# Head of a two-layer graph kernel on one core: where codes, casts, weights and the staging of h stand

## The chip, the cores and the metric

The kernel runs on one core of a Trainium2 chip. The metric is device time in microseconds, the median of three runs: 883.71 us (883.47 to 884.96). Engines are named as in the profile: PE (TensorE), DVE (VectorE), ACT (ScalarE), POOL (GpSimd) and SP, which only issues DMAs. SPq and ACTq are the DMA issues of SP and of ACT.

## The reference

4,096 nodes with 256 features, a 4096x4096 adjacency of zeros and ones, two graph layers, each followed by a residual and a layernorm:

```python
def reference(x, adj, ...):
    deg = jnp.maximum((adj != 0).astype(jnp.float32).sum(-1), 1.0)
    # layer 0: a_norm = (adj + I) scaled by deg on both sides; relu((a_norm @ x + x) @ W + b)
    x = _layernorm(x + _L0_gnn_ref(x, adj, deg[..., None], W, b), axis=-1)
    # layer 1: sums of neighbours, two sigmoid gates, attention over neighbours, second product with adj
    x = _layernorm(x + _L1_gnn_ref(x, adj, adj, W_sa, a_sa, W_gcnb, b_gcnb, Wa, ba, Wb, bb), axis=-1)
    return x
```

## The kernel before, in words

The 4,096 nodes are T = 32 tiles of 128. The change lies in the first third of the kernel, which ends at about 340 us of the span: layer 0 and the projections for layer 1. Nothing behind it is edited but two waits.

**Strips and codes.** The adjacency is read as 128 strips of 512 KB, 16 to a panel of 512 columns (eight panels). SP issues each strip into a ring of RING = 6 buffers; strip s waits for the cast of strip s-6. ACT (line 509) or DVE (line 791) casts a strip to 8-bit codes; `on_act(s)` says which. The codes of a panel, 2 MB, are later written to HBM by `codes_when_cast` (line 329), for layer 1. Before, they are issued when strip 16q+21 has been issued. SP is one queue in order: what stands behind a waiting issue waits too.

**The t loop (t = 0 to 32).** For each tile PE transposes x (`xt_step`, line 1334), multiplies the tile before it with W0 (`z_step`, line 1349), and from t = 14 adds one row block into all four sums of panel 0 (`pass0_rows`, eight matmuls of line 1366). ACT copies the transposes (`xt_copy`, line 517), the first twelve z and makes the high part of y (line 529). DVE copies the other z (line 804) and makes the low part (line 831). Before that DVE needs the largest |x| (`x_max`, line 798, one reduction for each chunk of x), from which the scale `sx_ready` comes. At t = WT_AT PE transposes `wrow` (line 1422), which waits for all ten small weight DMAs. At t = WNORM_AT PE adds the squared weights (line 1415), and DVE takes the norm (`weight_norm`).

**The sums.** After the t loop PE finishes tiles 0 to 3 with the remaining rows (128 matmuls), then does tiles 4 to 31, four to a panel: each is 64 matmuls of line 1366 in four quarters (`sum_tile`). Between the quarters stand one transpose of an earlier tile's x1 (`t_step`, line 1386) and one projection (`p_step`, line 1401, twelve matmuls). The first tile of a panel walks through all 16 of its strips.

**The tile chain.** DVE turns a finished sum into x1 (`degree`, `residual`, `stats`, `normalize`), with POOL for the power. After the projection ACT evicts q, g and the high part of h (`proj_copies`, lines 563 to 577), DVE makes the low part (`h_lo`, line 933) and ACT issues the tile's h to HBM (line 557). h is staged in `hst`, two buffers before the change: `proj_copies(n)` waits for the write of h(n-2) with `act.wait_ge(h_out[n % 2], ...)`. `p_step(n)` waits for `h_lo(n-1)`. All engines run their instructions in the order in which they are written.

**Casts between the tiles.** The t loop of ACT casts at each odd t from 11, that of DVE at each even t from 12. Then come three casts each, then single ones between the first tiles, and from n = 6 two on each engine per tile.

Of the kernel before, what the change touches and what calls it, by code (L numbers as in the profile page):

```python
# [14 lines left out]
P = 128  # L15
N = 4096
D = 256
T = N // P
# [15 lines left out]
WT_AT = 16  # L34
WNORM_AT = 23
WTS_AT = 4
WARM = 20
# [24 lines left out]
XCUT = (0, 2, 4, 8, 16, 24, 32)  # L62
# [28 lines left out]
def build(nc, x, adj, W0, b0, Wsa, asa, Wg, bg, Wa, ba, Wb, bb, out):  # L91
# [78 lines left out]
    hst = area("hst", [P, 2, 2, ROW], F16)  # L170
# [45 lines left out]
    with ExitStack() as ctx:  # L216
# [24 lines left out]
        panel_in, slb_in, h_out = (several(name, 2) for name in ("panel_in", "slb_in", "h_out"))  # L241
# [22 lines left out]
        on_act = lambda s: s % 2 == 0  # L264
# [17 lines left out]
        def h_place(n):  # L282

            return hst[:, n % 2] if n < T - 2 else fb[:, n]
# [23 lines left out]
        def _(sp):  # L308
# [23 lines left out]
            sp.dma_start(w0[:], W0.rearrange("(k p) d -> p k d", p=P)).then_inc(S["w0_in"], 16)  # L332
            for c in range(1, len(XCUT) - 1):
                t0, t1 = XCUT[c], XCUT[c + 1]
                sp.dma_start(xs[:, t0:t1, 0:D], x_view[:, t0:t1, :]).then_inc(x_in[c], 16)  # L335
            for s in range(NSTRIP):
                if s >= RING:
                    sp.wait_ge(S["cast_act" if on_act(s - RING) else "cast_dve"],
                               casts_until(s - RING)[0 if on_act(s - RING) else 1])
                qq, g = s // GS, s % GS  # L340
                sp.dma_start(strip[:, s % RING], adj_view[:, g * SJ:(g + 1) * SJ, qq * 2 * PW:(qq + 1) * 2 * PW]  # L341
                             ).then_inc(strip_in[s % RING], 16)
                if s == WTS_AT:
                    load_weights()
                if s >= RING and (s - RING) % GS == GS - 1:
                    codes_when_cast((s - RING) // GS)
# [19 lines left out]
            for c in range(NCH):  # L366
                upto = min((c + 1) * CH, T - 2)
                for i in range(2):
                    sp.wait_ge(h_out[i], 16 * upto // 2)
                sp.dma_start(fb[:, c * CH:upto].rearrange("p t k c -> p t (k c)"), hd[:, c * CH:upto, :]  # L370
                             ).then_inc(fb_in[c], 16)
# [124 lines left out]

        ACT_CASTS = [s for s in range(NSTRIP) if on_act(s)]
# [4 lines left out]
        def _(act):  # L502
# [27 lines left out]

            for t in range(T):
                xt_copy(t)
                if 1 <= t <= ZACT:
                    z_copy(t - 1)
                for i in split_at(t):
                    y_hi(i)
                if t >= 11 and t % 2 == 1:
                    cast(1)
# [13 lines left out]
            def proj_copies(n):  # L552

                t, p = n, n // 2
                if 0 < n < T - 1:
                    act.wait_ge(S["hlo_ready"], n)
                    act.dma_start(hd[:, n - 1, :], hst[:, (n - 1) % 2].rearrange("p k c -> p (k c)")
                                  ).then_inc(h_out[(n - 1) % 2], 16)
# [15 lines left out]
                if 2 <= n < T - 2:  # L574
                    act.wait_ge(h_out[n % 2], 16 * (n // 2))
# [12 lines left out]
            cast(3)  # L588
            x1t_copy(0)
            cast(1)  # L590
# [187 lines left out]
        def _(dve):  # L778
# [116 lines left out]
            z_scale()  # L895
            for t in range(ZACT, T):
                if t == WT_AT:
                    gate_columns()
                if t == WNORM_AT:
                    weight_norm()  # L900
                z_copy(t)
                for i in split_at(t):
                    y_lo(i)
                if t % 2 == 0:
# [7 lines left out]
                if t >= T - 4 and t % 2:  # L912
                    weight_parts((t - T + 4) // 2)
            for t in split_at(T):
                y_lo(t)
            cast(3)
# [93 lines left out]
            cast(1)  # L1010
            first_head(2)
            cast(2)
# [263 lines left out]
            for i in range(2):  # L1276
                dve.wait_ge(h_out[i], 16 * (T - 2) // 2)
# [141 lines left out]

# [211 lines left out]
```

## Time and profile before

| | us |
|---|---|
| median of three runs | 883.71 |
| the profiled execution, own time | 886.22 |
| its span | 884.1 |
| PE busy in the span | 859.0 |
| DVE busy | 670.8 |
| ACT busy | 570.6 |
| mean granted clock of PE | 0.992 |

The span runs from the first to the last instruction that the profiler recorded; the execution's own time is 2.1 us longer. Busy PE time is modelled from pipelined matmuls, so the stretches in which PE waits are the more telling reading. The rows below are read in this order: who PE waits for in the first third, at what clock it goes on, the order of time on PE, DVE and ACT, and what the DMA engines move in the same stretches.

### The profile page before, as it was taken

The page shows a single profiled execution, that of the slowest core. Times are in us where ns is not written, and L with a number is a line of the kernel's source. Part 1 is how long each engine was busy: PE and PEld are TensorE (multiplying, and loading weights), DVE is VectorE, ACT ScalarE, POOL GpSimd, SP SyncE. Part 2 cuts the span into 40 slices and gives each one's busy share as a digit, 9 for nine tenths or more (in the row PEclk, how much of TensorE's full clock was granted, in tenths as well). Part 3 has the DMA queues.
Part 4 walks back from the last instruction along what each step waited for, and adds up shares of the span by engine and source line. Part 5 has one row for each costly group of instructions (what it writes and reads, how often), then busy time and mean ns, then how long its engine had stood idle before and what let it go on. Part 6 is the DMA issues. An engine that isn't in the chain of part 4 may idle for free.

```text
span 884.1 us, 20460 instructions
## 1 busy us (share of the span) xinstructions
PE 859.0 (97%) x7579; PEld 756.9 (86%) x7579; DVE 670.8 (76%) x1182; ACT 570.6 (65%) x1214; POOL 178.2 (20%) x181
## 2 busy tenths in 40 slices
PE   8899799999999999999999999999999999999997
PEld 7778688888888887888788888888888888888886
DVE  5686566565666557998889988978978978879863
ACT  5663455454555327889877967967867867867831
POOL 1001233222232220110122022032032032032021
PEclk9999999999999999999999999999999999999999
DMA  9879799989989615101220220220220220220001
GB/s 319 286 263 324 256 397 381 373 302 342 357 300 365 234 42 212 57 5 52 78 79 1 77 77 0 77 77 0 77 77 0 77 77 0 77 77 0 25 25 36
DMA packets 66617, 130.01 MB, mean 147 GB/s; under 512 B 5464, under 2 KB 29056, under 8 KB 62080
## 3 DMA queue, kind: packets, MB, share of 16 engines
q1 hardware_dynamic: 57632, 120.87, 38.8%
q10 hardware_dynamic: 8928, 8.38, 2.8%
q8 instruction: 36, 0.59, 0.3%
q14 instruction: 21, 0.17, 0.1%
HBM read 99.87 MB, written 29.36 MB: 146 GB/s over the span
## 4 chain that ended last, share of the span: by engine, by line
PE 82%; DVE 5%; issue 4%; ACT 4%; SPq 2%; DMA 1%; POOL 0%; POOLq 0%; DVEq 0%; ACTq 0%
PE ps L1530 31%; PE ps L1366 25%; PE ps L1471 19%; PE ps L1401 5%; ACT ec L624 2%; DVE ec L1100 1%; PE ps L1349 1%; ACT em L633 1%; DMA sc<-in_L_gnn_bb_dram 1%; PE ps L1386 1%; SPq L341 1%; DVE em L1107 1%; SPq L335 1%; DVE dd L940 0%; DMA x1r<-x_scratch 0%
## 5 line engine op out<-in xcount | busy, mean ns | idle before, releaser
L1530 PE MATMUL ps<-fb,em 128*128 128x257 f16 x3072 | 347.5, 273 | 0.8 <-DVE em L1107 0.8
L1530 PEld LDWEIGHTS ps<-fb,em 128*128 128x128 f16 x3072 | 300.4, 98 | 38.6 <-issue 1.3
L1366 PE MATMUL ps<-y,codes 128*128 128x257 f16 x2048 | 238.4, 274 | 1.7 <-DVE codes L791 1.3
L1366 PEld LDWEIGHTS ps<-y,codes 128*128 128x128 fp8e4 x2048 | 200.6, 98 | 29.2 <-DVE codes L791 1.6
L624 ACT ACTIVATE ec<-slb,nsb 128x256 f32<-128x256 f32 x512 | 211.1, 496 | 0.0
L1107 DVE SCALAR_TENSOR_TENSOR em<-ec,em 128x2048 f16<-128x2048 f32 x64 | 147.4, 2303 | 22.7 <-ACT em L633 22.7
L633 ACT ACTIVATE em<-ec 128x2048 f16<-128x2048 f32 x64 | 122.0, 1908 | 65.4 <-PE ps L1530 57.2
L1100 DVE SCALAR_TENSOR_TENSOR ec<-ec,pan 128x2048 f32<-128x2048 f32 x64 | 147.3, 2301 | 2.6 <-issue 1.8
L1471 PE MATMUL ps<-zz,dd 128*128 128x256 f16 x768 | 89.4, 273 | 1.5 <-DVE t L1129 1.3
L458 POOL TENSOR_TENSOR sc<-sc,sc 128x2 f32<-128x2 f32 x15 | 38.5, 2569 | 246.2 <-DVE sc L1209 246.2
L1471 PEld LDWEIGHTS ps<-zz,dd 128*128 128x128 fp8e4 x768 | 75.0, 98 | 10.7 <-issue 2.0
L509 ACT ACTIVATE codes<-strip 128x1024 uint8<-128x1024 f32 x64 | 65.4, 1048 | 18.5 <-DMA strip<-in_adj_dram 17.5
L1471 PE MATMUL ps<-fa,pan 128*128 128x260 f16 x512 | 61.7, 279 | 3.4 <-DVE s L1138 2.1
L452 POOL TENSOR_TENSOR w<-w,bgb 128x512 f32<-128x512 f32 x16 | 27.7, 1732 | 184.6 <-DVE w L1167 184.6
L940 DVE SCALAR_TENSOR_TENSOR dd<-pan 128x512 uint32<-128x512 uint32 (+2 forms) x85 | 64.1, 814 | 0.0
L1471 PEld LDWEIGHTS ps<-fa,pan 128*128 128x128 fp8e4 x512 | 50.7, 99 | 11.7 <-issue 2.3
L1471 PE MATMUL ps<-fa,dd 128*128 128x260 f16 x512 | 59.6, 274 | 0.4 <-DVE m L1119 0.4
L1471 PEld LDWEIGHTS ps<-fa,dd 128*128 128x128 fp8e4 x512 | 49.9, 98 | 7.6 <-issue 0.9
L548 ACT ACTIVATE x1t<-ps 128x256 f16<-128x256 f32 x32 | 12.2, 382 | 66.0 <-PE ps L1386 66.0
L1401 PE MATMUL ps<-wps,x1t 128*128 128x256 f16 (+1 forms) x384 | 48.9, 278 | 4.1 <-issue 4.1
L791 DVE TENSOR_SCALAR codes<-strip 128x1024 uint8<-128x1024 f32 x64 | 43.8, 688 | 11.8 <-DMA strip<-in_adj_dram 11.8
L956 DVE TENSOR_SCALAR lnst<-ps 128x1 f32<-128x1 f32 x32 | 5.0, 156 | 60.7 <-PE ps L1366 60.6
(154 smaller groups left out, 765.1 us busy)
## 6 DMA issues: line engine op xcount, KB each, us to landing
strip<-in_adj_dram SPq DMA_DIRECT2D x128, 512.0 KB, 7.5
a_scratch<-codes SPq DMA_DIRECT2D x16, 1024.0 KB, 10.6
pan<-a_scratch SPq DMA_DIRECT2D x16, 1024.0 KB, 4.9
x_scratch<-x ACTq DMA_DIRECT2D x32, 128.0 KB, 5.2
x1r<-x_scratch SPq DMA_DIRECT2D x16, 256.0 KB, 2.8
h_scratch<-hst ACTq DMA_DIRECT2D x30, 136.0 KB, 5.4
out_dram<-ot SPq DMA_DIRECT2D x15, 256.0 KB, 2.2
fb<-h_scratch SPq DMA_DIRECT2D x3, 1088.0 KB, 8.7
```

The source lines that it names most:

```text
L458: pool.tensor_tensor(sc1[:, RS2], sc1[:, VE2], sc[:, MH2], ALU.pow).then_inc(S["yrstd_ready"], 1)
L509: act.activation(codes_of(s), strip_of(s), ACT.Copy, scale=float(EDGE - NONE), bias=float(NONE)).then_inc(S["cast_act"], 1)
L624: e_ = act.activation(ec[:, c % ER, jj, :], slb[:, slot, :], ACT.Exp, scale=-(1 - SLOPE), bias=nsb[:, jb:jb + 1])
L633: act.activation(em[:, c, 0], ec[:, c % ER], ACT.Copy, scale=MU / EDGE_VAL).then_inc(S["ehigh_ready"], 1)
L791: dve.tensor_scalar(codes_of(s), strip_of(s), float(EDGE - NONE), float(NONE), ALU.mult, ALU.add).then_inc(S["cast_dve"], 1)
L940: return dve.scalar_tensor_tensor(out=o, in0=b, scalar=0x7f7f7f7f, in1=a, op0=ALU.bitwise_and, op1=ALU.bitwise_xor)
L1100: dve.scalar_tensor_tensor(out=ec[:, c % ER], in0=ec[:, c % ER], scalar=1.0, in1=pan[:, slot, c * CH:(c + 1) * CH, :].bitcast(F8), op0=ALU ...
L1107: dve.scalar_tensor_tensor(out=em[:, c, 1], in0=ec[:, c % ER], scalar=MU / EDGE_VAL, in1=em[:, c, 0], op0=ALU.mult, op1=ALU.subtract).then ...
L1366: mm = pe.matmul(ACC(n), codes[:, qq % SLOTS, h, jb, e * P:(e + 1) * P].bitcast(F8), y[:, jb, part, 0:YC], start=(jb == 0 and part == 0), ...
L1401: mm = pe.matmul(b, x1t[:, n % 2, x_part, k * P:(k + 1) * P], wps[:, k, w_part, c0:c1], start=(k == 0 and x_part + w_part == 0), stop=(k = ...
L1471: mm = pe.matmul(ps[:, bank, 0:2 * c], a.bitcast(F8), g, start=(p == 0), stop=(p == NP - 1))
L1530: mm = pe.matmul(PH(2 * m + e)[:, 0:HC], em[:, c, e_part, i, e * P:(e + 1) * P], fb[:, jb, h_part, 0:HC], start=(jb == 0 and e_part + h_pa ...
```

## The change

Eight things are altered, all in the head:

1. The warm-up transposes go from 20 to 15, and x comes in eight chunks instead of six (the first two of one tile, the last two of four). W0's DMA is issued by ACT instead of SP.
2. `wrow`'s transpose and the weight steps behind it move from t = 16 to t = 20, the weight norm from t = 23 to t = 27. On DVE `gate_columns` and `weight_norm` move ahead of the casts of their tile.
3. ACT takes the odd strips, DVE the even ones, and ACT also all of strips 26 to 31. The casts of the t loops follow two lists: ACT at t = 13, 15, 19, 21 to 31, DVE once before the loop and at t = 14, 16, 20, 22 to 30.
4. After the t loops DVE casts four strips with `weight_parts(1)` between them, and none between the first heads; ACT casts seven, then two and one.
5. The codes of panel 0 are issued after strip 32 instead of 21, those of panel 1 after strip 43 instead of 37. The later ones stay at 16q+21.
6. `hst` has three buffers, and the waits and writes follow.
7. The waits at the end of the head for the h writes cover three semaphores.
8. The layout of the area of `hst`, `gb` and `fs` grows by one buffer.

```diff
-WT_AT = 16
-WNORM_AT = 23
+WT_AT = 20
+WNORM_AT = 27
-WARM = 20
+WARM = 15
+HRING = 3
+BOTH_AT = 26
-XCUT = (0, 2, 4, 8, 16, 24, 32)
+XCUT = (0, 1, 2, 4, 8, 16, 24, 28, 32)
-    hst = area("hst", [P, 2, 2, ROW], F16)
+    hst = area("hst", [P, HRING, 2, ROW], F16)
-        on_act = lambda s: s % 2 == 0
+        on_act = lambda s: s % 2 == 1 or BOTH_AT <= s < 2 * GS
...
-            sp.dma_start(w0[:], W0.rearrange("(k p) d -> p k d", p=P)).then_inc(S["w0_in"], 16)
+            CODES_AT = [2 * GS, 2 * GS + GS // 2 + RING // 2] + [q * GS + GS + RING - 1 for q in range(2, NQ - 1)]
-                if s >= RING and (s - RING) % GS == GS - 1:
-                    codes_when_cast((s - RING) // GS)
+                if s in CODES_AT:
+                    codes_when_cast(CODES_AT.index(s))
...
+        ACT_AT, DVE_AT = (13, 15, 19, 21, 23, 25, 27, 29, 31), (14, 16, 20, 22, 24, 26, 28, 30)
+            act.dma_start(w0[:], W0.rearrange("(k p) d -> p k d", p=P)).then_inc(S["w0_in"], 16)
-                if t >= 11 and t % 2 == 1:
+                if t in ACT_AT:
                     cast(1)
...
-                if 2 <= n < T - 2:
-                    act.wait_ge(h_out[n % 2], 16 * (n // 2))
+                if HRING <= n < T - 2:
+                    act.wait_ge(h_out[n % HRING], 16 * (n // HRING))
...
-            cast(3)
+            cast(7)
             x1t_copy(0)
-            cast(1)
+            cast(2)
             x1t_copy(1)
...
             z_scale()
+            cast(1)
             for t in range(ZACT, T):
-                if t == WT_AT:
+                z_copy(t)
+                if t == WT_AT - 1:
                     gate_columns()
-                if t == WNORM_AT:
-                    weight_norm()
-                z_copy(t)
                 for i in split_at(t):
                     y_lo(i)
-                if t % 2 == 0:
+                if t == WNORM_AT - 1:
+                    weight_norm()
+                if t in DVE_AT:
                     cast(1)
...
-                if t >= T - 4 and t % 2:
-                    weight_parts((t - T + 4) // 2)
+                if t == T - 1:
+                    weight_parts(0)
             for t in split_at(T):
                 y_lo(t)
-            cast(3)
+            cast(2)
+            weight_parts(1)
+            cast(2)
...
             first_head(1)
-            cast(1)
             first_head(2)
-            cast(2)
             first_head(3)
```

On PE, in the t loop, `xs` is x, `w_94` is W0 and `wrow` holds the rows of the gate weights. Before, the transpose of `wrow` is the sixth step of this piece, right behind the second row block of panel 0:

```order
L1366 MATMUL ps<-y,codes 128x257 x8
L1334 MATMUL ps<-ident,xs 128x128 x2
L1349 MATMUL ps<-w_94,xt 128x256 x2
L1422 MATMUL ps<-ident,wrow 128x8
L1366 MATMUL ps<-y,codes 128x257 x8
L1334 MATMUL ps<-ident,xs 128x128 x2
```

Now the same piece stands four tiles later:

```order
L1372 MATMUL ps<-y,codes 128x257 x8
L1340 MATMUL ps<-ident,xs 128x128 x2
L1355 MATMUL ps<-w_94,xt 128x256 x2
L1427 MATMUL ps<-ident,wrow 128x8
L1372 MATMUL ps<-y,codes 128x257 x8
L1340 MATMUL ps<-ident,xs 128x128 x2
```

Only its place moved: six row blocks of panel 0 stand ahead of it instead of two.

On SP, the issue of panel 0's codes (`a_scratch`) before, behind strip 21:

```order
L341 DMA strip<-in_adj_dram 128x2x512 [waits cast_act]
L341 DMA strip<-in_adj_dram 128x2x512 [waits cast_dve]
L329 DMA a_scratch<-codes 128x8192 [waits cast_dve,cast_act]
L329 DMA a_scratch<-codes 128x8192
L341 DMA strip<-in_adj_dram 128x2x512 [waits cast_act]
```

And now, behind strip 32 (the row "x2" is strips 31 and 32, the row "x5" strips 33 to 37):

```order
L344 DMA strip<-in_adj_dram 128x2x512 [waits cast_dve]
L344 DMA strip<-in_adj_dram 128x2x512 [waits cast_act] x2
L332 DMA a_scratch<-codes 128x8192 [waits cast_dve,cast_act]
L332 DMA a_scratch<-codes 128x8192
L344 DMA strip<-in_adj_dram 128x2x512 [waits cast_act] x5
L344 DMA strip<-in_adj_dram 128x2x512 [waits cast_dve]
```

Ten strips of panel 1 and the first one of panel 2 have moved ahead of the 2 MB, and strips 33 to 37 wait for ACT alone.

On ACT, from the last steps of the t loop to the second tile, before:

```order
L529 ACTIVATE y<-zf,sc 128x256 [waits zf_dve] x2
L509 ACTIVATE codes<-strip 128x2x2x256 [waits strip_in4]
L509 ACTIVATE codes<-strip 128x2x2x256 [waits strip_in0]
L509 ACTIVATE codes<-strip 128x2x2x256 [waits strip_in2]
L548 ACTIVATE x1t<-ps 128x256 [waits x1t_done]
L550 DMA x_scratch<-x_61 128x256 [waits x1_ready]
L509 ACTIVATE codes<-strip 128x2x2x256 [waits strip_in4]
```

And now:

```order
L533 ACTIVATE y<-zf,sc 128x256 [waits zf_dve] x2
L513 ACTIVATE codes<-strip 128x2x2x256 [waits strip_in1]
L513 ACTIVATE codes<-strip 128x2x2x256 [waits strip_in3]
L513 ACTIVATE codes<-strip 128x2x2x256 [waits strip_in5]
L513 ACTIVATE codes<-strip 128x2x2x256 [waits strip_in1]
L513 ACTIVATE codes<-strip 128x2x2x256 [waits strip_in2]
L513 ACTIVATE codes<-strip 128x2x2x256 [waits strip_in3]
L513 ACTIVATE codes<-strip 128x2x2x256 [waits strip_in4]
L553 ACTIVATE x1t<-ps 128x256 [waits x1t_done]
L555 DMA x_scratch<-x_61 128x256 [waits x1_ready]
L513 ACTIVATE codes<-strip 128x2x2x256 [waits strip_in5]
L513 ACTIVATE codes<-strip 128x2x2x256 [waits strip_in0]
```

Four more casts (strips 19 to 28 in all) stand ahead of the copy of the first transposed x1, and two instead of one behind it.

## Rows read from the trace of the kernel before

**Rows 1.** Waits of PE, 0 to 330 us: line, releaser, total, times, longest.

```profile
PE ps L1401 <- issue: 4.1, 1, 4.1
PE ps L1422 <- DMA sc<-in_L_gnn_bb_dram: 2.7, 1, 2.7
...
PE ps L1366 <- DVE codes L791: 1.3, 1, 1.3
PE ps L1349 <- ACT xt L517: 1.0, 3, 0.4
PE ps L1386 <- DVE x L990: 0.9, 1, 0.9
PE ps L1415 <- DVE zf L804: 0.5, 1, 0.5
PE ps L1366 <- DVE y L831: 0.4, 1, 0.4
```

**Rows 2.** Windows: stretch, length, five engines' busy time, granted clock, DMA, GB/s.

```profile
30.60:34.00 3.40, 3.40 (x14) 2.55 (x12) 0.08 (x1) 1.29 (x3) 0.00 (x0) 0.50 0.95 358
102.30:105.70 3.40, 2.89 (x14) 2.05 (x15) 3.12 (x10) 0.10 (x1) 0.72 (x1) 0.51 0.30 112
```

**Rows 3.** PE in order of time: start, length, instruction, [idle before <- releaser].

```profile
1.78 4.53 PE L1325 MATMUL ps<-ident 128*128 128x128 f32 x20 [1.78 <-POOL ident L416]
...
29.99 0.22 PE L1422 MATMUL ps<-ident,wrow 8*128 8x8 f32 x1 [2.74 <-DMA sc<-in_L_gnn_bb_dram]
...
34.68 0.38 PE L1334 MATMUL ps<-ident,xs 128*128 128x128 f32 x2
...
36.64 0.38 PE L1334 MATMUL ps<-ident,xs 128*128 128x128 f32 x2
...
102.81 2.75 PE L1401 MATMUL ps<-wps,x1t 128*128 128x262 f16 x12 [4.06 <-issue]
...
108.38 0.44 PE L1386 MATMUL ps<-ident,x 128*128 128x128 f32 x2 [0.95 <-DVE x L990]
...
129.35 1.49 PE L1401 MATMUL ps<-wps,x1t 128*128 128x262 f16 x12
```

**Rows 4.** DVE in time: the last x reduction, tile 6's low x1t.

```profile
16.90 2.29 DVE L798 TENSOR_REDUCE sc<-xs 128x1 f32<-128x2048 f32 x1 [0.58 <-DMA xs<-in_x_dram]
...
126.44 0.42 DVE L946 SCALAR_TENSOR_TENSOR x1t<-ps,x1t 128x256 f16<-128x256 f32 x1
```

**Rows 5.** ACT and its DMA issues in time, around two waits.

```profile
90.59 0.64 ACTq L557 DMA_DIRECT2D h_scratch<-hst  x1
...
101.56 0.20 ACT L576 ACTIVATE hst<-q 128x1 f16<-128x1 f32 x1 [4.23 <-DMA h_scratch<-hst]
...
121.64 1.06 ACT L509 ACTIVATE codes<-strip 128x1024 uint8<-128x1024 f32 x1 [1.93 <-DMA strip<-in_adj_dram]
```

**Rows 6.** Windows, the last two numbers: DMA share and GB/s.

```profile
35.00:40.00 5.00, 5.00 (x36) 4.22 (x35) 4.24 (x13) 3.88 (x9) 0.00 (x0) 1.00 0.62 221
...
80.00:90.00 10.00, 8.68 (x79) 7.50 (x78) 7.95 (x25) 2.85 (x9) 2.58 (x5) 1.00 0.76 245
...
100.00:110.00 10.00, 6.24 (x43) 4.80 (x44) 6.36 (x18) 4.93 (x12) 2.89 (x5) 0.83 0.45 151
110.00:120.00 10.00, 10.00 (x94) 8.90 (x92) 6.78 (x21) 5.97 (x14) 1.82 (x3) 1.00 1.02 378
```

**Rows 7.** The page, part 6: DMA issues, count, size, median us to landing.

```profile
strip<-in_adj_dram SPq DMA_DIRECT2D x128, 512.0 KB, 7.5
a_scratch<-codes SPq DMA_DIRECT2D x16, 1024.0 KB, 10.6
...
h_scratch<-hst ACTq DMA_DIRECT2D x30, 136.0 KB, 5.4
```

**Rows 8.** Waits of SP's queue, 0 to 330 us: who held strips.

```profile
SPq L341 <- ACT codes L509: 136.3, 36, 10.5
```

**Rows 9.** SP's queue in order of time: the codes of panel 1.

```profile
88.59 0.98 SPq L329 DMA_DIRECT2D a_scratch<-codes  x2
```

More of the change, by code:

```diff
@@ L240, in build @@
         codes_out, x1_out = several("codes_out", SLOTS), several("x1_out", X1RING)
-        panel_in, slb_in, h_out = (several(name, 2) for name in ("panel_in", "slb_in", "h_out"))
+        panel_in, slb_in = (several(name, 2) for name in ("panel_in", "slb_in"))
+        h_out = several("h_out", HRING)
         fb_in, x1r_in, out_sent = several("fb_in", NCH), block_sem("x1r_in"), block_sem("out_sent")
@@ L282, in h_place @@
         def h_place(n):
-            return hst[:, n % 2] if n < T - 2 else fb[:, n]
+            return hst[:, n % HRING] if n < T - 2 else fb[:, n]
         def differences(slot, op, p0, p1):
@@ L367, in _ @@
                 upto = min((c + 1) * CH, T - 2)
-                for i in range(2):
-                    sp.wait_ge(h_out[i], 16 * upto // 2)
+                for i in range(HRING):
+                    sp.wait_ge(h_out[i], 16 * len(range(i, upto, HRING)))
                 sp.dma_start(fb[:, c * CH:upto].rearrange("p t k c -> p t (k c)"), hd[:, c * CH:upto, :]
@@ L556, in proj_copies @@
                     act.wait_ge(S["hlo_ready"], n)
-                    act.dma_start(hd[:, n - 1, :], hst[:, (n - 1) % 2].rearrange("p k c -> p (k c)")
-                                  ).then_inc(h_out[(n - 1) % 2], 16)
+                    act.dma_start(hd[:, n - 1, :], hst[:, (n - 1) % HRING].rearrange("p k c -> p (k c)")
+                                  ).then_inc(h_out[(n - 1) % HRING], 16)
                 act.wait_ge(S["proj_done"], n + 1)
@@ L1275, in _ @@
             read_52(0, first=True)
-            for i in range(2):
-                dve.wait_ge(h_out[i], 16 * (T - 2) // 2)
+            for i in range(HRING):
+                dve.wait_ge(h_out[i], 16 * len(range(i, T - 2, HRING)))
             add_52(0, first=True)
```

## The prediction, made before the changed kernel was run

> **What bounds the kernel now.** I read the waits of PE first, since PE is busy for 859 of 884 us and nothing can be won that is not one of its waits, its clock, or work that it is spared. In the first 330 us PE waits seven times for something that the change touches [rows 1]: 4.1, 2.7, 1.3, 1.0, 0.9, 0.5 and 0.4 us. From 110 us on PE is busy without a gap up to 330 us (the last window of [rows 6] is the first such one), so the change can be worth only what stands ahead of 110 us, and whatever is saved there must not come back as a wait behind it. The second view is the granted clock: after each of the two long waits it falls to 0.5 (1.2 GHz) for 3.4 us [rows 2], and after that it is back at 1.0. The third is the order of time on PE, DVE and ACT, which says what each wait is made of.
>
> The 4.1 us stand as "issue" on PE, but PE was held by p_step(3), which needs h_lo(2). ACT had done everything up to the eviction of h(2) and stood 4.23 us before 101.56 waiting for the write of h(0) out of the same buffer [rows 5]. That write was issued at 90.59 and needed 10.9 us, where the 30 writes have a median of 5.4 [rows 5, 7]; 2 MB of panel 1's codes had been issued 2 us before it [rows 9].
>
> **The change, part by part.** Each gain below is for PE, which sets the end here.
>
> *Warm-up and x.* Twenty transposes take 4.53 us, or 0.227 each [rows 3]; five fewer are 1.1 us. W0 leaves SP's queue, and the first x chunk is half as large, so x is there. But the first y waits for the largest |x|, whose last reduction (8 tiles, 2.29 us) starts at 16.90 when x has landed [rows 4]. Two chunks of four tiles take half of it each; the first runs mostly while the second lands, but it starts behind the 2.29 us of the chunk before, so about 0.4 us is saved there. ACT's order then also loses a cast ahead of the first y. The gain at the first row block lies between 0.4 and 1.1; I take **0.8**, nearer the upper end because one of ACT's short waits (0.4, [rows 1]) lies in the same place.
>
> *The weights.* PE idles 2.74 us before `wrow`'s transpose, for a DMA landing at 29.99 [rows 3], and the half clock from 30.60 costs another 3.4 / 2 = 1.7 [rows 2]. A step of the t loop is 36.64 - 34.68 = 1.96 us [rows 3]. Four steps later and 0.8 earlier, the transpose is reached at 29.99 - 2.74 - 0.8 + 4 x 1.96 = 34.3 us. The weights keep their place in SP's queue with the same bytes ahead of them, so they land near 30: a cover of 4.3 us. Gain 2.7 + 1.7 = **4.4** (4.0 to 4.4).
>
> *The weight norm.* The step from the squares to the norm's matmul is three tiles as before, so the 0.5 us on line 1415 [rows 1] stays. What followed it (0.4 on the next z, [rows 1], since DVE did a cast before the norm) goes: **+0.4** (0 to 0.6). At the end of the loop ten small weight instructions of DVE now stand three tiles from the end instead of seven, ahead of the low y on which PE already waits 0.4 [rows 1]. I put **-0.3** (-1.0 to +0.4).
>
> *Codes of panel 0 and the casts.* 2 MB at 378 GB/s [rows 6, 7] are 5.5 us of the DMA engines, a strip is 1.39. Ten strips of panel 1 now pass ahead of them. The casts of the t loop free the buffers at the loop's own pace, so I expect these strips some 6 us earlier than before, which is also by how much PE comes earlier (0.8 + 4.4 + 0.4 - 0.3 = 5.3): they are neither the gain nor the loss. The 1.3 us that PE waits for a cast of DVE [rows 1] stem from two DVE casts behind the third head. These go to ACT, whose last one (strip 31) stands behind one x1t copy and `proj_copies(0)`. I estimate its end 2.9 us behind the end of t_step(1) (a cast is 1.06 [rows 5], the copies before it under 2); PE needs it after 28 of 32 matmuls at 0.11, 3.1 us behind. Cover 0.2 us. Gain **1.3** (0.5 to 1.3).
>
> *The ring of three.* `proj_copies(2)` waits no more. The write of h(0) is then asked for only by `proj_copies(3)`, one projection and 64 matmuls later. The wait of 4.06 goes and with it the half clock that made twelve matmuls take 2.75 us where they take 1.49 [rows 3]: 4.06 + 1.3 = **5.4** (4.0 to 5.5). Next late is what stands now: the 0.95 before t_step(4) [rows 3], DVE's chain of head(4) and h_lo(3). With a shorter p_step(3) DVE's part ends relatively later: **-0.3** (-1 to 0).
>
> Sum so far: 0.8 + 4.4 + 0.4 - 0.3 + 1.3 + 5.4 - 0.3 = 11.7 us.
>
> *What comes back: the DMA engines.* Panel 2's strips have to be there 11.7 us sooner, and from 110 to 120 us the engines are at a share of 1.02 [rows 6]. Before, the last cast of ACT for panel 2 starts at 121.64 when its strip lands [rows 5]; DVE's is one strip later, 123.0. The bytes up to that strip are the same after the change. What can be made up is idle time of the engines: against 378 GB/s, 221 over 35 to 60 us (taking the row shown for the 25 us) is 10.4 us idle, 245 over 80 to 90 is 3.5, 151 over 100 to 110 is 6.0: 20 us. After: two strips a step of the loop are 1.05 MB in 3.93 us = 267 GB/s, so some 24 us x 0.29 = 7 idle there, and about 3 where strip 38 waits for DVE's cast of strip 32, which stands behind forms_lo(0). So 20 - 10 = 10 us are made up, and the last strip lands at 113.2 (110.5 to 116.5). It is now ACT's. From the start of ACT's last cast to the low x1t of tile 6 it took 126.86 - 121.64 = 5.2 us [rows 4, 5], with a little waiting in it: 5.0. So p_step(6), which needs that, can start at 118.2; without any wait it would start at 129.35 - 11.7 = 117.65 [rows 3]. Taking also the writes of x1 and h that fall between, I put **-1.2** (0 to -4). After that the engines gain on PE: a panel is 16 x 1.39 + 5.5 + 2.9 for x1 and h = 30.6 us against 34.3 of PE (four tiles of 64 matmuls, a projection and a transpose, 8.6 each). The steady casts wait little; SP waits for casts for 136.3 us [rows 8], not casts for SP.
>
> Net 11.7 - 1.2 = 10.5 us, which shifts the whole rest of the kernel. The profiled execution took 886.22 with a span of 884.1; the median of the runs is 883.71, and the sum is a difference, so it goes to the median: **873.2 us**.
>
> A rule weighed against it. Row: the write of h(0), on ACT's queue, landed 10.9 us after its issue, behind codes on SP's queue [rows 5, 9]. The Trainium skill, DMA: Bandwidth & Descriptors, section Queues, rings and completion order, says that each DMA engine round-robins between queue rows by the packet, and by that alone the write would have taken the usual 5.4 us, nobody would have waited, the ring would gain nothing, and the sum would be 10.5 - 5.4 = 5.1, or 878.6; the trace disagrees, with 10.9 us. The same section says that a semaphore's increment lands only behind every earlier write of that engine across its queues; the trace agrees, and by it the sum stays at 10.5.
>
> **The rivals.**
>
> *A: no time comes back* (the strips land as early as PE asks). For it: 10 us of made-up idle time is only 0.5 us short of what tile 8 needs. Time 883.7 - 11.7 = 872.0, or 871 with the upper ends of the small terms.
>
> *B: more comes back.* Codes written slower than 5.5 us, the two narrow covers (0.2 us at strip 31, none at p_step(3)) not held, and a wait at tile 8 that is long enough for the clock to fall: 1.3 at 4.06 or 2.74 us of idleness, not after 1.3 [rows 1, 2]; the case between is not in these rows. Price 4 + 1.7 on top of A: 877 to 879.
>
> *C: the ring only moves the wait.* If h(0) still takes 10.9 us when `proj_copies(3)` asks for it, PE waits there. The write is issued 6.6 us earlier than before (the terms up to there), at 84.0, and asked for about 1 us behind p_step(3), at 102.81 + 2.75 + 1.0 - 12.0 = 94.6 [rows 3, 5]: 10.6 us later, so by that row 0.3 us are missing, and if panel 1's codes came as close as before, up to 4.1 + 1.3. Time 874 to 878.6. Against it: panel 1's codes leave behind strip 43, after the question.
>
> *D, the other side: the DMA engines become the bound.* Place: strips 33 to 47 with both panels' codes and the writes of x1 and h, 13.5 MB, which must pass between about 77 and 114 us. Rows for 100 to 110 and 80 to 90 show 151 and 245 GB/s [rows 6], but with queues standing empty. If mixing reads with 2 MB of writes brought the mean to 250, it would take 54 us instead of 36, the last strip would be 18 us late, and the kernel would end near 890; it is slower than before once the mean is under 290 GB/s. Against it: 378 GB/s at a share of 1.02 [rows 6].
>
> **How the numbers follow.** Forecast (873.2, alone 871.5 to 875.5) 0.58; A 0.15; B 0.14; C beyond the forecast's range 0.05; D 0.04; the remaining 0.04 is a change of the same size as the noise, where DMA takes back nearly all. The range reaches down over A and up through B: 870.5 to 878.5. A measurement of this kernel can tell about 0.2% (1.8 us) from no change. Faster by more 0.94, within it 0.02, slower 0.04.
>
> **What would show it.** Right: the waits of PE before 110 us lose the lines of `wrow` (2.7), of "issue" at the projection (4.1) and of the cast (1.3), and the half clock of 30.6 and of 102.3 us is gone; ACT shows no wait for `h_scratch`; t_step(4) still waits about 1 us; a new wait of 1 to 2 us of PE at a projection near 118 us, with ACT's casts of strips 45 and 47 waiting for their DMA just ahead. Wrong: a wait at `wrow` (weights later than 34), waits at strip 31 or p_step(3), or no wait near 118 (A) or over 3 us there (B).

## The result, and the profile after

The changed kernel took **878.60 us** in the median of five runs (876.64 to 879.03), beside 883.47 us for the kernel before (five runs, 882.71 to 884.96): a ratio of 0.9939, interval 0.9925 to 0.9954. I had forecast 873.2 us with a range of 870.5 to 878.5. The kernel is faster, but by about half of what I had said, and the time lies 0.1 us above the range. Later runs of both kernels on another chip gave 877.87 us and 884.84 us, a ratio of 0.9926 (0.9911 to 0.9942), so the gain is 5 to 7 us, not 10.5. Two of the twelve executions with the weights at their old place, below, took 2,322 and 5,135 us and are left out of its numbers. The profiled execution of after took 878.33 us with a span of 876.2 us; that of before 886.22 and 884.1.

The waits of PE from 0 to 340 us in after (line and tile, releaser, total us, times, longest) answer to [rows 1].

```profile
PE ps L1407 <- DVE x1t L954: 2.9, 2, 2.3
PE ps L1331 <- POOL ident L419: 1.8, 1, 1.8
PE ps L1392 <- DVE x L998: 1.2, 1, 1.2
...
PE ps L1372 <- DVE y L836: 0.7, 1, 0.7
PE ps L1421 <- DVE zf L809: 0.4, 1, 0.4
```

Three lines of [rows 1] are gone as planned: "issue" at the projection (4.1), the weights (2.7) and the cast (1.3). The top line is new: 2.9 us at the projection, in two pieces, for the low half of x1t. The order of time on PE in after shows where (start, length, instruction, [idle before <- releaser]); it answers to [rows 3].

```profile
1.78 3.46 PE L1331 MATMUL ps<-ident 128*128 128x128 f32 x15 [1.78 <-POOL ident L419]
...
34.12 0.22 PE L1427 MATMUL ps<-ident,wrow 8*128 8x8 f32 x1
...
58.27 14.25 PE L1372 MATMUL ps<-y,codes 128*128 128x257 f16 x128 [0.69 <-DVE y L836]
...
86.29 1.49 PE L1407 MATMUL ps<-wps,x1t 128*128 128x262 f16 x12
...
91.35 1.49 PE L1407 MATMUL ps<-wps,x1t 128*128 128x262 f16 x12
...
95.79 0.44 PE L1392 MATMUL ps<-ident,x 128*128 128x128 f32 x2 [1.19 <-DVE x L998]
...
109.11 1.50 PE L1407 MATMUL ps<-wps,x1t 128*128 128x262 f16 x12 [0.56 <-DVE x1t L954]
...
120.19 2.77 PE L1407 MATMUL ps<-wps,x1t 128*128 128x262 f16 x12 [2.32 <-DVE x1t L954]
...
130.31 1.49 PE L1407 MATMUL ps<-wps,x1t 128*128 128x262 f16 x12
```

The same steps in before that did not stand among [rows 3], from the same view:

```profile
64.07 14.25 PE L1366 MATMUL ps<-y,codes 128*128 128x257 f16 x128 [0.36 <-DVE y L831]
...
93.53 1.49 PE L1401 MATMUL ps<-wps,x1t 128*128 128x262 f16 x12
...
120.76 1.49 PE L1401 MATMUL ps<-wps,x1t 128*128 128x262 f16 x12
...
137.93 1.49 PE L1401 MATMUL ps<-wps,x1t 128*128 128x262 f16 x12
```

Subtracting the starts step by step gives how far ahead after is, and this is the best single reading of the case:

| step of PE | before | after | ahead by | I had summed |
|---|---|---|---|---|
| first sums of panel 0 | 64.07 | 58.27 | 5.80 | 5.3 |
| p_step(2) | 93.53 | 86.29 | 7.24 | 6.6 |
| p_step(3), after the wait for h | 102.81 | 91.35 | 11.46 | 10.7 |
| t_step(4) | 108.38 | 95.79 | 12.59 | 11.7 |
| p_step(5) | 120.76 | 109.11 | 11.65 | 11.7 |
| p_step(6) | 129.35 | 120.19 | 9.16 | 11.2 |
| p_step(7) | 137.93 | 130.31 | 7.62 | 10.5 |

Up to t_step(4) after is 0.9 us better than my sum. Between t_step(4) and p_step(7) it gives back 12.59 - 7.62 = 5.0 us where I had put 1.2; from there to the end the lead hardly changes (884.1 - 876.2 = 7.9).

What PE waits for there is read from ACT's order of time in after and from the chain of waits between 90 and 124 us (start, length, what), which here runs through strips and their casts. The rows of ACT answer to the last one of [rows 5].

```profile
101.88 1.06 ACT L513 ACTIVATE codes<-strip 128x1024 uint8<-128x1024 f32 x1 [3.40 <-DMA strip<-in_adj_dram]
...
112.89 1.06 ACT L513 ACTIVATE codes<-strip 128x1024 uint8<-128x1024 f32 x1 [5.46 <-DMA strip<-in_adj_dram]
115.57 1.06 ACT L513 ACTIVATE codes<-strip 128x1024 uint8<-128x1024 f32 x1 [1.62 <-DMA strip<-in_adj_dram]
```

```profile
95.32 6.54 DMA strip<-in_adj_dram
...
102.96 12.59 DMA strip<-in_adj_dram
...
115.57 0.33 ACT codes L513
...
120.19 2.77 PE ps L1407 x12
```

The three casts are those of strips 41, 45 and 47, and ACT is idle for 10.5 us ahead of them, each time for a strip. Strip 47, the last of panel 2, took 12.59 us from its issue to its landing, where the strips of after have a median of 7.4. The projections' copies stand behind these casts on ACT, DVE's low x1t behind the copies, and p_step(6) behind that. On the page, the idle time of ACT's casts rose from 18.5 to 34.2 us. The windows of after (stretch, length, busy time of PE, PEld, DVE, ACT and POOL, granted clock, DMA share, GB/s) answer to [rows 6] and [rows 2]:

```profile
35.00:60.00 25.00, 23.95 (x165) 20.05 (x164) 20.45 (x59) 17.07 (x36) 2.61 (x3) 1.00 0.71 235
80.00:90.00 10.00, 10.00 (x93) 8.71 (x91) 6.92 (x19) 5.68 (x18) 2.96 (x6) 1.00 1.01 387
90.00:100.00 10.00, 8.77 (x78) 7.33 (x77) 8.97 (x24) 6.11 (x15) 4.11 (x6) 1.00 0.91 277
104.00:116.00 12.00, 11.44 (x105) 9.98 (x103) 5.55 (x18) 4.14 (x10) 1.27 (x2) 1.00 1.03 405
120.00:123.40 3.40, 3.21 (x16) 2.27 (x17) 3.33 (x10) 2.60 (x6) 0.71 (x2) 0.51 1.08 424
```

From 104 us on the DMA engines are full (share 1.03, 405 GB/s). The last row is the half clock: PE ran at 1.2 GHz for 3.4 us behind its idle time of 2.32 us, which costs another 1.54 us by the table (9.16 - 7.62). The two such stretches of [rows 2] are gone.

### The profile page after: what moved, and what is told of

It is laid out like the page before. It is cut to its first block, busy times and chain, and to the rows that moved or that the text cites. A ratio compares the mean times of both kernels' runs of the same rounds, so it can differ in the third digit from the quotient of the medians.

```text
span 876.2 us, 20454 instructions
## 1 busy us (share of the span) xinstructions
PE 855.4 (98%) x7574; PEld 754.2 (86%) x7574; DVE 670.0 (76%) x1181; ACT 573.6 (65%) x1217; POOL 178.1 (20%) x181
## 4 chain that ended last, share of the span: by engine, by line
PE 81%; DVE 6%; ACT 4%; issue 4%; DMA 2%; POOL 1%; ACTq 0%; POOLq 0%; DVEq 0%; SPq 0%
PE ps L1535 30%; PE ps L1372 23%; PE ps L1476 19%; PE ps L1407 5%; PE ps L1355 3%; DMA strip<-in_adj_dram 2%; DVE ec L1106 2%; ACT ec L629 2%; DVE em L1113 1%; ACT em L638 1%; DVE dd L948 1%; PE ps L1392 1%; PE ps L1340 1%; PE ps L1331 0%; POOL sc L461 0%
## 5 line engine op out<-in xcount | busy, mean ns | idle before, releaser
L513 ACT ACTIVATE codes<-strip 128x1024 uint8<-128x1024 f32 x67 | 68.7, 1048 | 34.2 <-DMA strip<-in_adj_dram 33.2
L1476 PEld LDWEIGHTS ps<-zz,dd 128*128 128x128 fp8e4 x768 | 75.0, 98 | 10.6 <-issue 2.0
L674 ACT ACTIVATE ot<-sg,sc 128x256 f32<-128x256 f32 x30 | 16.4, 593 | 52.4 <-POOL sc L465 52.4
L553 ACT ACTIVATE x1t<-ps 128x256 f16<-128x256 f32 x32 | 12.2, 381 | 56.0 <-PE ps L1392 56.0
## 6 DMA issues: line engine op xcount, KB each, us to landing
a_scratch<-codes SPq DMA_DIRECT2D x16, 1024.0 KB, 10.9
```

The costliest lines, as they stand in the source:

```text
L513: act.activation(codes_of(s), strip_of(s), ACT.Copy, scale=float(EDGE - NONE), bias=float(NONE)).then_inc(S["cast_act"], 1)
L1476: mm = pe.matmul(ps[:, bank, 0:2 * c], a.bitcast(F8), g, start=(p == 0), stop=(p == NP - 1))
```

## The experiments

All are timed against the kernel before in the same hour on the same chip. "Before" there had medians of 885.26, 884.84 and 885.31 us on three chips (23, 12 and 19 runs), 1.4 to 1.8 us above its first five runs. Ratios across chips are better compared than times. An h ring of three is called ring 3 below.

### Before, once more

> The kernel before, unchanged, for its spread from run to run. Theory: the profiled run of before (886.22 us, mean granted clock 0.992) was long for that kernel: it held 2.5 us that its timed runs (median 883.47) do not have, since one of the three stretches at half clock, worth 1.7 us each, or a part of the 4.23 us wait for h_scratch comes in some executions only. Then the runs here show clocks of 0.994 to 0.996 beside 883.0 to 884.0 us, and a new profile shows one or two stretches at half clock instead of three, or a wait at the projection clearly under 4.06 us. Rival: the profiled run differs only in what lies around the span; then the clocks are 0.992 again and the three stretches and the 4.06 us are all there, with a span near 881.5 us.

Measured: 885.62 us (882.45 to 887.38, twelve runs), ratio 0.9996 (0.9982 to 1.0010). Its new profile (span 885.2), waits of PE:

```profile
PE ps L1401 <- issue: 3.7, 1, 3.7
PE ps L1422 <- DMA sc<-in_L_gnn_bb_dram: 3.6, 1, 3.6
```

Both half-clock stretches of [rows 2] are there again, and the two waits add up to 7.3 us where [rows 1] have 6.8. The third stretch of my theory lies behind the head, at 426 to 430 us in both profiles of before, and over it the lead of after grows by only 0.3 us, to the 7.9 at the end. Each of the fourteen profiles of this document has one of two things there: the clock falls behind a wait of 2.1 us, as here and in seven others, or it holds and PE waits 1.12 to 1.16 us some 19 us later, as in both profiles of after and in four others. So the theory fell in its main part: the profiled run was no odd one, the first five runs were short ones. Before varies by some 5 us from run to run, with a mean granted clock from 0.990 to 0.997 over all its runs; after varies by 2.6 (876.64 to 879.26 over eleven runs).

### After, once more

> The kernel after, unchanged, on the chip and in the hour of the other runs, as their yardstick: 877.5 to 879.5 us is expected, as in its first five runs (median 878.6). Before, in that hour, ran at 885.3 us (882.65 to 887.66, 23 runs) and not at 883.5. Theory: before varies from run to run and after does not, so that the gain here is 6 to 7.5 us, near the 7.9 us between the two profiled runs. Rival: this chip is slower for both, and after comes to 880 us or more.

Measured: 877.87 us (877.36 to 879.26, six runs), ratio 0.9926 (0.9911 to 0.9942): 7.0 us by the medians of that chip, as the theory said. Its profile has the same wait at p_step(6), slightly longer, and no half clock behind it. The row of PE and the window:

```profile
121.11 1.50 PE L1407 MATMUL ps<-wps,x1t 128*128 128x262 f16 x12 [2.64 <-DVE x1t L954]
```

```profile
120.00:124.00 4.00, 2.89 (x27) 2.56 (x28) 3.79 (x12) 3.88 (x9) 1.41 (x2) 1.00 1.08 411
```

Over both chips, four of the eleven runs show a mean clock of 0.999 (876.64 to 877.87 us) and seven of 0.997 (877.87 to 879.26 us). That the clock's fall at p_step(6) comes in some executions only is shown by the two profiles; that it is what parts these two groups is not shown, since a fall behind the head would lower the mean as well.

### The ring alone, and the codes alone, on the kernel before

> The kernel before with one part of the change alone: the h ring of three. The prediction's term: PE's wait of 4.06 us (3.7 us in the second profile) at the projection at 102.8 us goes, with 1.3 us of half clock, so 4 to 5.4 us less than before's 884.8 to 885.3 us, less 1.2 us that comes back at the strips: 880.6 to 882.1 us. Rival 1 (the ring only moves the wait): panel 2's strips land where they did, and DVE's x1t waits for the casts of strips 43 to 47 instead; the waits at p_step(5) and p_step(6) grow by 2 to 3 us, and the time is 883 to 884.5 us. Rival 2 (as in the pair with the codes in before's order, 881.1 against 879.2): 2 us less, 882.8 to 883.3 us.

```diff
-    hst = area("hst", [P, 2, 2, ROW], F16)
+    hst = area("hst", [P, HRING, 2, ROW], F16)
...
-                if 2 <= n < T - 2:
-                    act.wait_ge(h_out[n % 2], 16 * (n // 2))
+                if HRING <= n < T - 2:
+                    act.wait_ge(h_out[n % HRING], 16 * (n // HRING))
```

Measured: 880.52 us (878.59 to 883.36, eight runs), ratio 0.9949 (0.9932 to 0.9966): 4.8 us by the medians. No wait for h_scratch is left on ACT, none of PE at the projections up to 330 us, and of the half clock only the stretch at the weights. By itself, on this kernel, the term of the ring was right. The write of h(0) still took 10.6 us in this profile; nobody waited for it.

> The kernel before with one part of the change alone: panel 0's codes go out behind strip 32 and panel 1's behind strip 43 (before: 21 and 37). Theory (the order of the codes alone takes the wait for h away, as a ring of two cost nothing in the kernel after): no wait for h_scratch of over 0.5 us on ACT, no wait of 3.7 to 4.1 us at a projection, and a part of it comes back as waits at p_step(5) and p_step(6): 881.5 to 883.5 us. The prediction's term for the codes: 1.3 us, all by itself, with the wait for h still there: 883.5 to 884.0 us.

```diff
-                if s >= RING and (s - RING) % GS == GS - 1:
-                    codes_when_cast((s - RING) // GS)
+                if s in CODES_AT:
+                    codes_when_cast(CODES_AT.index(s))
```

Measured: 882.39 us (880.78 to 885.40, twelve runs), ratio 0.9972 (0.9960 to 0.9985): 2.9 us. With a ring of two, and the codes moved alone, ACT's wait for h_scratch is gone as well: the write of h(0) took 5.1 us. Two new waits stand further on, on PE:

```profile
119.57 0.44 PE L1387 MATMUL ps<-ident,x 128*128 128x128 f32 x2 [1.31 <-DVE x L991]
124.44 1.50 PE L1402 MATMUL ps<-wps,x1t 128*128 128x262 f16 x12 [0.91 <-DVE x1t L947]
```

So the order of the codes alone removes the wait that I had given to the ring, and brings some of it back at the strips. My 1.3 us for the codes were for another thing, a cast.

SP's queue shows why something comes back. First before, behind the codes of panel 1 [rows 9], then after:

```profile
96.17 1.32 SPq L341 DMA_DIRECT2D strip<-in_adj_dram  x2
```

```profile
97.66 1.32 SPq L332 DMA_DIRECT2D a_scratch<-codes  x2
99.03 17.99 SPq L344 DMA_DIRECT2D strip<-in_adj_dram  x10
```

In the old order the 2 MB leave while the ring of strips stands still: before issues them at 88.59 us, and strip 38, which needs the cast of strip 32, only at 96.17. With ring 3 alone it is 88.06 and 95.64. The engines write the codes in that pause. In the new order the pause stays, nearly empty, and the codes go out between strips 43 and 44: at 102.36 us with the codes moved alone, with the next strip at 103.47. From 92 to 96 us the DMA share is 1.00 with ring 3 alone and 0.50 with the codes alone. Over 90 to 100 us the engines move this much in before, where after has 277 GB/s:

```profile
90.00:100.00 10.00, 8.75 (x80) 7.48 (x77) 4.66 (x12) 5.05 (x16) 2.16 (x4) 1.00 1.00 362
```

### The ring of two in the kernel after, under both orders of the codes

> The kernel after with h ring of two instead of three. The prediction's term: without the third place ACT waits for h(0)'s write, PE loses 4.06 us plus 1.3 us of half clock, and with the give-back of before the time rises by 2 to 5.4 us, to 880.6 to 884.0 us. Rival (the order of the codes alone removed that wait): in the kernel after h(0) is issued at 83.34 us, behind panel 0's codes, which have landed by 83.4 us, and it has landed when ACT asks at about 89.97 us; then a ring of two costs 0 to 0.5 us, and the time is 878.3 to 879.3 us.

```diff
-HRING = 3
+HRING = 2
```

Measured: 878.36 us (877.77 to 878.78, six runs), ratio 0.9922 (0.9907 to 0.9937), against 0.9926 for after itself: the ring is worth nothing measurable here. PE's waits are those of after, the two pieces at the projection included:

```profile
109.37 1.50 PE L1407 MATMUL ps<-wps,x1t 128*128 128x262 f16 x12 [0.61 <-DVE x1t L954]
...
120.44 2.77 PE L1407 MATMUL ps<-wps,x1t 128*128 128x262 f16 x12 [2.32 <-DVE x1t L954]
```

> The kernel after with the codes of all panels sent where before sent them (behind strips 21, 37, 53, ...), and the h ring of three. Theory (the waits of before came from the order alone: h(0) queued behind panel 0's codes, then panel 1's codes behind strip 37): strips 38 to 41 land later by the 2 MB of panel 1's codes, about 5 us, so a wait of 1 to 5 us comes at p_step(4) or p_step(5) and then less is left at p_step(6); 878 to 882 us. The prediction's term (a ring of three takes the wait for h away whatever the order): no wait at the projection of tile 2 or 3. Rival: the strips up to 37 come early enough to pay for it, the waits at p_step(5) and p_step(6) shrink, and the time is 876 to 878 us.

```diff
-            CODES_AT = [2 * GS, 2 * GS + GS // 2 + RING // 2] + [q * GS + GS + RING - 1 for q in range(2, NQ - 1)]
+            CODES_AT = [q * GS + GS + RING - 1 for q in range(NQ - 1)]
```

Measured: 879.18 us (877.33 to 879.46, six runs), ratio 0.9932 (0.9917 to 0.9948). With a ring of three the two orders are not told apart.

> The kernel after with the codes sent where before sent them and an h ring of two: of the change only the weights, the x chunks and the casts are left. Against the same order with a ring of three it prices the ring alone. The prediction's term: ACT waits some 4 us for h_scratch, PE idles 4.06 us at a projection and loses 1.3 us at half clock, and 1.2 us of it comes back, so 4 to 5.4 us above the ring of three. Rival 1 (the other edits have moved the codes away from h(0) already): within 0.5 us of the ring of three. Rival 2 (the strips of panel 2 set the time at p_step(5) and p_step(6) in either): the wait for h is there, but the two waits behind it go, and the difference is 0.5 to 2 us.

This is the same edit, with HRING = 2 beside it. Measured: 881.10 us (880.18 to 883.58, seven runs), ratio 0.9959 (0.9944 to 0.9974). The wait for h is back on ACT, but short; on PE it stands as 1.51 us of "issue":

```profile
99.50 0.21 ACT L581 ACTIVATE hst<-q 128x1 f16<-128x1 f32 x1 [1.81 <-DMA h_scratch<-hst]
```

```profile
76.40 0.69 PE L1392 MATMUL ps<-ident,x 128*128 128x128 f32 x2 [3.56 <-DVE x L998]
94.02 1.49 PE L1407 MATMUL ps<-wps,x1t 128*128 128x262 f16 x12 [0.69 <-issue]
...
100.76 1.49 PE L1407 MATMUL ps<-wps,x1t 128*128 128x262 f16 x12 [1.51 <-issue]
```

With the old order the ring is worth 881.10 - 879.18 = 1.9 us, with the new order nothing: two edits, one wait. The old order has a cost of its own in this kernel: PE waits for x of the first tile, 3.56 us here and 2.99 with ring 3. In both, the waits at p_step(5) and p_step(6) are gone, as the pause on SP's queue has it; the loss was paid earlier. Panel 0's codes behind strip 32 with panel 1's behind strip 37, which might keep both gains, was not run.

### The weights back at their old place

> The kernel after with the weights prepared where before had them (WT_AT 16, WNORM_AT 23). The prediction's term: PE waits 2.7 us for the gate weights again and loses 1.7 us to half clock, all of it on the path, so 878.6 + 4.4 = 883.0 us (882.0 to 883.5). Rival (the strips of panel 2 cap what the stretch before them can win): sums start 4.4 us later while the strips land where they did, so the waits of 0.56 and 2.32 us and the half clock at p_step(6) go, and the net loss is 0.2 to 1.5 us, 878.8 to 880.1 us.

```diff
-WT_AT = 20
-WNORM_AT = 27
+WT_AT = 16
+WNORM_AT = 23
```

Measured: 883.7 us (878.90 to 885.68, ten runs), ratio 0.9978 (0.9962 to 0.9994). Against 0.9926 for after this is 0.52% or 4.6 us: the term of the weights (4.4) was right. The order of time on PE, with one window of the granted clock and one row of ACT under it:

```profile
30.75 0.27 PE L1427 MATMUL ps<-ident,wrow 8*128 8x8 f32 x1 [3.96 <-DMA sc<-in_L_gnn_bb_dram]
...
126.94 1.94 PE L1407 MATMUL ps<-wps,x1t 128*128 128x262 f16 x12 [2.78 <-DVE x1t L954]
```

```profile
30.75:34.15 3.40, 3.40 (x14) 2.74 (x15) 0.72 (x3) 0.78 (x2) 0.00 (x0) 0.50 0.83 320
```

```profile
122.32 1.06 ACT L513 ACTIVATE codes<-strip 128x1024 uint8<-128x1024 f32 x1 [1.59 <-DMA strip<-in_adj_dram]
```

The rival fell, and how is of use: the sums start later, but the wait at p_step(6) is 2.78 us all the same. The strips don't land at fixed times. SP loads a strip when a cast has freed its buffer, the casts stand among PE's steps, and so a delay ahead of the sums moves the strips as well: the sums start 6.6 us later than in after (64.89), and strip 47 is cast 6.75 us later.

### Panel 1's codes behind strip 47, and all codes late

> The kernel after with one change: panel 1's codes go out behind strip 47 instead of behind strip 43, so that nothing but strips is on SP's queue while panel 2 is read. Theory (panel 2's second half is late because 2 MB of codes run beside it): strips 44 to 47 land 4 to 5 us sooner, PE's waits of 0.56 us at p_step(5) and 2.32 us at p_step(6) and the half clock behind them (1.3 us) go, and the time is 878.6 - 4.2 = 874.4 us (873.8 to 875.5). Rival 1 (the bytes must come anyway): the wait moves to panel 3, at tile 12, and the time stays at 878 to 879 us. Rival 2 (the low rate of 96 to 102 us, about 245 GB/s, is what makes the strips late, whatever else is in the queue): strips 41 to 43 land where they did, a wait of 0.5 to 1 us stays at p_step(5), and the time is 875.5 to 877 us.

```diff
-            CODES_AT = [2 * GS, 2 * GS + GS // 2 + RING // 2] + [q * GS + GS + RING - 1 for q in range(2, NQ - 1)]
+            CODES_AT = [2 * GS, 3 * GS - 1] + [q * GS + GS + RING - 1 for q in range(2, NQ - 1)]
```

Measured: 878.61 us (877.32 to 879.58, six runs), ratio 0.9924 (0.9908 to 0.9939), no different from after. The waits at p_step(5) and p_step(6) are gone, and one of the same size has come two steps later; the row is from PE's order of time:

```profile
137.87 1.64 PE L1407 MATMUL ps<-wps,x1t 128*128 128x262 f16 x12 [2.65 <-DVE x1t L954]
```

Rival 1 was right in its mechanism (the bytes must come anyway), with the wait at tile 8 and not at tile 12.

> The kernel after with the codes of panels 1 to 6 sent later: behind strips 58, 70, 82, 94, 106 and 117 in place of 43, 53, 69, 85, 101 and 117. Theory (between about 104 and 137 us the DMA engines are full at 390 to 430 GB/s and 2 MB of codes are 5.2 us of that; the strips alone are due, the codes are not): PE's waits of 0.56 us at p_step(5) and 2.32 us at p_step(6) and the half clock go, no 2.65 us wait comes at p_step(8) as with the codes behind strip 47, and the time is 878.4 - 4 = 874.4 us (873.5 to 875.5). Rival (the bytes only wait): codes 1 and 2 come close together and the wait moves to panel 4, whose casts need panel 1's codes to have landed; 877.5 to 880 us.

```diff
-            CODES_AT = [2 * GS, 2 * GS + GS // 2 + RING // 2] + [q * GS + GS + RING - 1 for q in range(2, NQ - 1)]
+            CODES_AT = [32, 58, 70, 82, 94, 106, 117]
```

Measured: **874.85 us** (873.53 to 875.55, five runs), ratio 0.9885 (0.9867 to 0.9902), 3.0 us less than after on the same chip; the two ranges don't meet. The edit moves the codes of panels 1 to 5 (behind strips 43, 53, 69, 85 and 101 in after); those of panels 0 and 6 stay. The waits of PE from 0 to 340 us, ACT's cast of strip 47 and two windows:

```profile
PE ps L1392 <- DVE x L998: 1.2, 1, 1.2
...
PE ps L1407 <- DVE x1t L954: 0.4, 2, 0.2
```

```profile
110.24 1.06 ACT L513 ACTIVATE codes<-strip 128x1024 uint8<-128x1024 f32 x1 [1.88 <-DMA strip<-in_adj_dram]
```

```profile
116.00:128.00 12.00, 12.00 (x112) 10.67 (x110) 7.30 (x20) 5.93 (x13) 2.32 (x3) 1.00 0.95 326
128.00:140.00 12.00, 12.00 (x112) 10.71 (x110) 6.63 (x21) 5.97 (x18) 3.13 (x5) 1.00 1.00 356
```

In after the engines moved 408 GB/s from 116 to 128 us and PE worked for 9.7 of the 12 us; here they move 326 and PE works for all 12. Strip 47 is cast at 110.24 us where after has 115.57: 5.3 us, about what 2 MB take at 378 GB/s [rows 6]. So the wait at p_step(6) was the price of 2 MB of codes that are not due until panel 4 takes their buffer. This is the version that beats both kernels.

### Two casts of DVE earlier

> The kernel after with DVE's casts of strips 32 and 34 moved ahead of first_head(3) and of forms_lo(0). Theory (the ring of six strips stands still at 88 to 92 us because strip 32, landed long before, is cast only at 89.1 us behind forms_lo(0), and the DMA engines move 239 GB/s there instead of 390): the strips behind come 1.5 to 2.5 us sooner, the wait of 2.3 to 2.6 us at p_step(6) falls to about 0.5 us, and the wait of 1.19 us at t_step(4) falls by the 0.7 us of a cast that no longer stands ahead of it: 877.9 - 2.5 = 875.4 us (874.5 to 876.5). Rival (DVE's two casts hold up x1 of tiles 2 and 3, on which PE's t_step waits): PE waits 0.7 to 1.4 us at t_step(3) or at the projection behind it, and the time is 877 to 878.5 us.

```diff
             first_head(2)
+            cast(1)
             first_head(3)
-            forms_lo(0)
             cast(1)
+            forms_lo(0)
             x1t_lo(3)
             h_lo(2)
-            cast(1)
             head(4)
```

Measured: 879.18 us (877.97 to 880.36, six runs), ratio 0.9933 (0.9915 to 0.9951): no gain. The windows tell why; the second is 369 GB/s in after.

```profile
88.00:92.00 4.00, 4.00 (x38) 3.54 (x37) 2.99 (x10) 2.49 (x8) 0.00 (x0) 1.00 1.06 399
92.00:96.00 4.00, 2.59 (x24) 2.05 (x21) 3.12 (x8) 3.10 (x8) 2.89 (x5) 1.00 0.61 230
```

The gap at 88 to 92 us was closed, and the same gap opened at 92 to 96: the ring then stood at ACT's casts, three of which (94.24, 2.94 us) follow proj_copies(3). PE's waits are 1.21 us at p_step(5) and 2.52 at p_step(6), and t_step(4) waits 1.59. My theory fell, since a ring that two engines free moves at the pace of the later one; the rival's mechanism (x1 of tiles 2 and 3 held up) isn't in the trace either.

> The kernel after with the late codes (strips 58, 70, 82, 94, 106, 117) and with the two casts of DVE moved ahead. Theory (the late codes alone took PE's waits at p_step(5), p_step(6) and the half clock, 874.85 us; what the casts add is the 0.7 us at t_step(4) and the last 0.2 us at p_step(5)): 873.8 to 874.3 us. Rival (the casts hold up x1 of tiles 2 and 3): 874.8 to 876 us.

This is the edit above with the codes at 32, 58, 70, 82, 94, 106 and 117. Measured: 874.94 us (874.34 to 875.39, five runs), ratio 0.9884 (0.9866 to 0.9903): the late codes are all of it, the casts add nothing. PE has a wait of 1.34 us at 247.18 that the late codes alone have at 0.22.

## Why the prediction was right or wrong, point by point

*Warm-up, x and weights.* Right. The sums start 5.80 us sooner, I had 5.3. The transpose of `wrow` is reached at 34.12 us without a wait; I had worked out 34.3. The reverse experiment prices the weights at 4.6 us.

*Weight norm and late low y.* The 0.5 us at the norm stayed, as I said (0.4 in after), the 0.4 on the next z is gone, and the wait on the low y rose from 0.36 to 0.69: the -0.3 was right.

*Codes of panel 0 and the casts.* The 1.3 us came (5.80 at the first sums, 7.24 at p_step(2)), and strip 31's narrow cover held: no wait for codes stands on PE. What I missed is that the same order makes the ring superfluous.

*The ring of three.* The size was right and the attribution wrong. The lead grew by 12.59 - 7.24 = 5.35 us between p_step(2) and t_step(4), I had 5.4 - 0.3. But in this kernel it is the codes' order that brings it: with a ring of two the time is the same. I put the whole wait down to the ring, although my own row showed the cause: the write of h(0) was issued 2 us behind panel 1's codes, and these were moved by the change. The write of h(0) itself took 10.9 us beside these codes, and 10.6 with a third buffer; away from them it took 5.1 (codes moved alone) and 3.2 (after). On the rule that I weighed there (the Trainium skill, DMA: Bandwidth & Descriptors, section Queues, rings and completion order): if arbitration by the packet kept other queues' codes from holding up a small write, moving the codes would not have taken the wait away. It did, and so these runs speak against that rule as the whole account; the section's second rule, that a semaphore's increment waits for the engine's earlier writes on other queues, agrees with them. That the alternative I gave for it was 878.6 is chance, since the 5.4 us were won.

*t_step(4).* 1.19 us in place of 0.95; I had -0.3 for this. Right.

*What comes back.* **This is the step that failed.** I put 1.2 us, it was 5.0. By the table 0.94 us go up to p_step(5), 0.56 of them its wait; 2.49 up to p_step(6), with its wait of 2.32; and 1.54 behind it, at half clock. I had the last strip of panel 2 land at 113.2, with 10 us of the engines' idle time made up. ACT's cast shows 115.57. The idle time by the same reckoning against 378 GB/s is 25 x (1 - 235/378) = 9.5 us from 35 to 60 us, where I had 7, and 10 x (1 - 277/378) = 2.7 from 90 to 100, where I had 3. That is 12.2 in place of 10, and the 2.2 us are nearly the 2.4 by which the strip is late. So the term that was mis-sized is the idle time that the engines make up: 7.8 us in place of 10, above all because the engines moved 235 GB/s from 35 to 60 us and not the 267 of two strips in 3.93 us. And what stood right ahead of strips 44 to 47 were the codes that the change had moved there; sent later, they took the wait with them (874.85 us). From the cast to p_step(6) it took 4.6 us (I had 5.0). The other part is the clock. My rows showed that it fell behind waits of 2.74 and 4.06 us and not behind 1.3, and I left the case between to rival B; 2.32 us were enough here.

*The rivals.* It went as B had it in effect (877 to 879, chance 0.14), though not by the narrow covers, neither of which gave way; the wait long enough for the clock to fall, which it also named, came. A fell. C did not occur: the codes had left h's way, and even a ring of two waits for nothing. D did not occur as such, but the DMA engines did set PE's pace between t_step(4) and p_step(7), for 5 us and not for the 1.2 that I had allowed.

*From the profile to the median.* Also a miss. A difference between profiled executions was carried over to the median of three runs, 883.71. The profiled executions differ by 7.9 us, the medians of one hour by 7.0, and the first five runs by 4.9. Before has longer waits, and two falls of the clock in the head in either profile, and it spreads more widely; three runs of it were too few to stand for its middle.

*A reading of the rows that was off.* [rows 1] count nine waits and not seven, since the 1.0 us are three; nothing hangs on it.

*Still open.* Why the engines' share is 0.91 between 90 and 100 us at only 277 GB/s; that the rate is low fits the pause in which SP issues few strips. Why the clock falls behind a wait in one execution and not in the next.

## What to carry to other kernels

When several edits take a wait away, ask for each whether another has removed its cause already; a term priced alone may be paid once, not twice. When PE gains some 10 us on a stretch in which a transfer queue is nearly full, put down by the row which bytes are due by which step, and send what is not yet due (here 2 MB of codes) after what is: that was worth 3 us, and moving it by a few strips nothing. Before moving a transfer, look at what stands still where it is now: the old place of these codes was a pause of the strips. And let the base be as many runs as the spread asks for.

## What the runs showed of the hardware

The granted clock falls behind a wait in some executions and not in others, with the same kernel and nearly the same wait: behind 2.32 us at p_step(6) it fell to 0.51 (profile of after), behind 2.64 us it stayed at 1.00 (its second profile). I had expected it to follow from the length of the wait alone. A fall is not always lost time: the one at p_step(6), with 3.4 us at 1.2 GHz, cost 1.54 us, while the one at 426 us in before cost little, since the kernel waits later on where it stays away.

A write of 136 KB on ACT's queue, issued beside 2 MB of codes on SP's, took 10.9 us [rows 5, 9] and made ACT wait 4.23. With a third buffer it took 10.6 and nobody waited; with the codes issued elsewhere it took 5.1.
